# A graph kernel's gather on one core: VectorE's loop over six batches becomes a loop over two, and ScalarE copies finished tiles in a loop

## The reference

```python
# layer 1: gather rows of the features, weight, sum by destination
agg = segment_sum(layernorm(x)[src] * edge_weight[:, None], dst, 6250)
x = x + einsum('ni,oi->no', agg, W) + b
# layer 2: the half of the nodes with the largest router value go through gelu(sel @ w1 + b1) @ w2 + b2
x = x + ffn_of_chosen(layernorm(x))
# layer 3: 16 relations, each with its own 256x256 weight, a gate, then the same sum by destination
msg = einsum('nf,rfo->rno', h, weight)[rel_type, src] * norm * sigmoid(gate)
x = x + relu(segment_sum(msg, dst, 6250))
# layer 4: 8 experts of 256 -> 1024 -> 256, the top 2 of each node
x = x + experts(layernorm(x))
```

## Time and profile before

| | |
|---|---|
| device time, three runs | 4026.05, 4010.23, 4010.8 us; median 4010.8 us |
| profiled execution: span from first to last instruction | 3402.6 us (the page gives no other time of it) |
| between that span and the median of the runs | 608.2 us |
| instructions executed in the span | 59974 |
| PE, DVE, ACT, POOL busy | 2615.4, 1733.1, 723.6, 1869.7 us |
| granted TensorE clock, mean | 0.902 of full speed |
| the two gathers (POOL's first to last tile) | 78.7 to 1069.4 us, and to 2662.8 us for the second |

### The profile page before, as it was taken

The page is one execution under the profiler, slowest core; times in us unless marked ns, Lnnn a source line. Parts: engine busy times, 40 slices in busy tenths (PEclk is TensorE's granted clock), DMA queues, the critical chain, the costliest instruction groups (busy, mean ns, idle before and its releaser), DMA issues. The chain is left out here.

```text
span 3402.6 us, 59974 instructions
## 1 busy us (share of the span) xinstructions
PE 2615.4 (77%) x14271; PEld 1921.6 (56%) x14272; DVE 1733.1 (51%) x5663; ACT 723.6 (21%) x1907; POOL 1869.7 (55%) x1915
## 2 busy tenths in 40 slices
PE   7688888887777799999655555564555389999997
PEld 6577777776665344444344444443444267767774
DVE  6455545454554655555355454544544544545553
ACT  4121111111110233333211010000000233333332
POOL 1777777777774000000377777777777245555554
PEclk9899999998999899999888888777777689999998
DMA  7333333333332444444545454555544623222232
GB/s 224 110 113 113 113 111 111 113 113 113 110 113 67 173 197 192 188 191 194 194 141 155 151 154 142 152 154 151 146 146 146 241 59 48 45 45 48 45 48 33
DMA packets 175589, 434.08 MB, mean 128 GB/s; under 512 B 41712, under 2 KB 103792, under 8 KB 169232
## 3 DMA queue, kind: packets, MB, share of 16 engines
q0 software_dynamic: 97072, 236.21, 26.9%
q1 hardware_dynamic: 57424, 183.78, 14.1%
q10 hardware_dynamic: 21008, 13.24, 1.3%
HBM read 275.05 MB, written 158.04 MB: 127 GB/s over the span
## 5 line engine op out<-in xcount | busy, mean ns | idle before, releaser
L776 POOL DMA_INDIRECT g_msg<-table,idx x1564 | 1517.3, 970 | 518.8 <-issue 476.5
L848 PE MATMUL psum<-g_msg,g_hot 128*128 x3328 | 967.4, 456 | 593.0 <-SPq L719 358.1
L848 PEld LDWEIGHTS psum<-g_msg,g_hot 128*128 128x128 f32 x3328 | 756.5, 233 | 789.5 <-issue 654.5
L796 DVE TENSOR_SCALAR g_hot<-iota,g_cols 128x128 f32<-128x128 f32 x1664 | 450.1, 364 | 31.9 <-DVE g_cols L793 30.5
L1908 POOL DMA_INDIRECT out<-ex_y,ex_to x112 | 206.0, 1839 | 253.9 <-DMA out<-ex_y,ex_to 165.3
L768 POOL MEMSET g_origin<- 128x256 f32 x1 | 0.3, 313 | 590.8 <-POOLq L1359 590.8
L1594 PE MATMUL psum<-wrel_halves,t_xhi 128*128 128x512 f16 x784 | 298.2, 380 | 1.7 <-DVE t_row L1475 1.7
L1595 PE MATMUL psum<-wrel_halves,t_xhi 128*128 128x512 f16 x784 | 298.1, 380 | 0.0
L1596 PE MATMUL psum<-wrel_halves,t_xlo 128*128 128x512 f16 x784 | 298.1, 380 | 0.0
L1475 DVE TENSOR_SCALAR t_row<-psum,t_gate 128x256 f32<-128x256 f32 x392 | 171.2, 479 | 233.7 <-PE psum L1596 231.7
L2074 PE MATMUL psum<-w,ex_ghi 128*128 x784 | 260.6, 382 | 6.7 <-DVE ex_y L1983 6.4
(11 more groups left out here) (353 smaller groups left out, 3231.7 us busy)
## 6 DMA issues: line engine op xcount, KB each, us to landing
table<-t_row SPq DMA_DIRECT2D x48, 2048.0 KB, 6.3
g_msg<-table,idx POOLq DMA_INDIRECT x1564
piece_stage<-in_w SPq DMA_DIRECT2D x32, 512.0 KB, 5.7
w_halves<-piece_halves SPq DMA_DIRECT2D x32, 512.0 KB, 3.4
w<-w_halves SPq DMA_DIRECT2D x8, 2048.0 KB, 22.6
rows<-sc_row ACTq DMA_DIRECT2D x50, 128.0 KB, 2.2
out<-acc ACTq DMA_DIRECT2D x49, 128.0 KB
table<-t_row SPq DMA_DIRECT2D x24, 256.0 KB, 2.5
```

Source lines behind the costliest of these rows:

```text
L776: pool.indirect_dma_start(out=msg[:, at:at + D], out_offset=None, in_=table, in_offset=bass.IndirectOffsetOnAxis(ap=t[f"idx{g}"][:, n:n + ...
L796: last = nc.vector.tensor_scalar(hot[b][:, k * P:(k + 1) * P], t["iota32"][:, :], c3[:, k, where:where + 1], c3[:, k, weight:weight + 1], ...
L848: pe.matmul(ps, hot[b % PAIR][:, k * P:(k + 1) * P], msg[:, bass.ds(slot_at[k], D)], start=False, stop=False, skip_group_check=True).then_ ...
```

## The change

DVE's loop over the pieces becomes a loop of three turns within a loop: each inner turn makes two batches, runs one slot, and by two If tests halves the even piece in the first turn and the odd piece in the third. ACT's eight nested copies become one, under an If, and behind it a loop over the second to the eighth finished window, entered only where two or more windows have ended. Slot numbers are read with a load that tests its bounds on the chip. PE masks the two kinds of register value on which it waits with 1023.

```diff
     def slot_number(eng, m):
-        _, (n,) = nc.values_load_multi_w_load_instructions(slot_at(m, 0, 1), engines=[eng.engine], min_val=0, max_val=WINDOWS,
-                                                           skip_runtime_bounds_check_because=sure)
-        return n
+        return eng.value_load(slot_at(m, 0, 1), min_val=0, max_val=WINDOWS)
...
                 with dve.Fori(kind * turns, (kind + 1) * turns) as i:
-                    for k in range(2 * EACH):
-                        batch(2 * EACH * i + k, k % PAIR)
-                        if k % EACH == 1:
-                            pieces.halve(dve, kind, 2 * i + k // EACH, k // EACH)
-                        if k % 2:
-                            slots(dve, follow.vector, EACH * i + k // 2, tiles=True)
+                    with dve.Fori(0, EACH) as j:
+                        turn = EACH * i + j
+                        for b in range(PAIR):
+                            batch(PAIR * turn + b, b)
+                        with dve.If(j <= 0):
+                            pieces.halve(dve, kind, 2 * i, 0)
+                        with dve.If(j >= EACH - 1):
+                            pieces.halve(dve, kind, 2 * i + 1, 1)
+                        slots(dve, follow.vector, turn, tiles=True)
...
-                    pe.wait_ge(tiles_in, code[MSG_TILES])
+                    pe.wait_ge(tiles_in, code[MSG_TILES] & 1023)
                     for k in range(BATCH):
                         if k % BANKS == 0:
-                            pe.wait_ge(bank_free, code[BATCH + k // BANKS] + 1)
+                            pe.wait_ge(bank_free, (code[BATCH + k // BANKS] & 1023) + 1)
...
-            def close_from(k, m, start, end):
-                with act.If(end - start >= k + 1):
-                    _, (n,) = nc.values_load_multi_w_load_instructions(
-                        t["closed"][0:1, bass.ds(m, 1)], engines=[act.engine], min_val=0, max_val=WINDOWS - 1 - k,
-                        skip_runtime_bounds_check_because=sure)
-                    close(n + k)
-                    if k + 1 < BATCH:
-                        close_from(k + 1, m, start, end)
+            def close_all(m, start, end):
+                with act.If(end - start >= 1):
+                    n = act.value_load(t["closed"][0:1, bass.ds(m, 1)], min_val=0, max_val=WINDOWS - 1)
+                    close(n)
+                    with act.If(end - start >= 2):
+                        with act.Fori(1, BATCH) as k:
+                            with act.If(end - start - k >= 1):
+                                n = act.value_load(t["closed"][0:1, bass.ds(m, 1)], min_val=0, max_val=WINDOWS - 2)
+                                close(nc.s_assert_within(n + k, 0, WINDOWS - 1))
```

More of the change, by code:

```diff
@@ L895, in _ @@
                         t["closed"][0:1, bass.ds(m, 2)], engines=[act.engine], min_val=0, max_val=WINDOWS, skip_runtime_bounds_check_because=sure)
-                    close_from(0, m, start, end)
+                    close_all(m, start, end)
                 if follow:
```

## The result

| | before | changed |
|---|---|---|
| device time, median of four runs each on one chip | 4010.5 us (4004.6 to 4026.1) | 4074.3 us (4067.0 to 4082.7) |
| ratio, 95% interval | | 1.0162 (1.0135 to 1.0188) |
| profiled execution: device time, span | not given, 3402.6 us | 4082.7, 4080.8 us |
| granted clock, mean | 0.902 | 0.812 |
| instructions executed | 59974 | 61714 |

The change makes the kernel 64 us slower, 1.6%; I had forecast 4012.8. The profiled execution of the changed kernel is one of its timed runs, and its device time is its span and 1.9 us. So next to nothing lies around a span, and the trace of before that I read, at 3402.6 us, was not like the runs that I had set beside it.

A forecast was written before the change was run, and what follows sets the result against it. Prediction: POOL's issuing of indirect DMAs bounds both gathers; gather ends add +1.1 and +0.85, about +2 us, on the 3402.6 us span, giving 3404.6; with 608.2 carried over, 4012.8 us, range 4004 to 4022.

The forecast's parts named there:

- The sum's last step: Whole kernel: 608.2 us between profiled span and median run time, added unchanged to the forecast span of 3404.6 us.
- "to spare" figures: Gathers at POOL's pace: DVE has 6.3 us a turn, ACT waits 7.4 a copy, PE's release margin 3.6.
- the rival of 0.09: Around the span: the 608.2 us shrink with the program's 8.9% fewer instructions, -54 us, to 3957; chance 0.09.
- against 6.3 us to spare: 0: DVE's loop in the gathers: 0.8 us a turn added, hidden in 6.3 us of slack, cost 0.
- weighed the fetch: DVE's gather loop: old 236 instructions, now 98, not fetched again each turn, so a smaller loop gains 0.
- Net one ahead of the first matmul and one ahead of the fifth: PE's masks in each batch: register operations exposed 0.27 us a turn on 18.2, POOL stall taken as 0.
- forecast up to 30, under 6: Sign in the changed profile: SP's waits for PE before a release, up to 30 us in sum, each under 6.
- the slot number's check of 0.34: PE at gather 0's end: each of three loads that become checked costs 0.34 us with handovers.
- PE becomes the pace: Gather 0 turns: PE instead of POOL sets the pace, 20 us needing +1.8 us a turn, 4031; chance 0.05.
- +1.1 us at gather 0: End of gather 0: three checked loads, 1.0 us, plus 0.1 to 0.2 of masks delay PE's slot and first count.
- the 0.85 forecast: End of gather 1: three checked loads on ACT, 0.7 us, with PE's masks 0.85.
- ScalarE's loop: 0: ACT's copies: the new loop never runs; each close's checked load, some 0.24 us, hides in a 7.4 us wait.

The follow-up runs named there:

- unrolled_dve: Changed kernel with VectorE's loop over the pieces written out entirely, no loop: 3407.3 us, 1.0001 to the kernel before.
- old_both: Changed kernel with VectorE's old loop and ScalarE's old nested copies, keeping checked loads and PE's masks: 4093.6 us, 1.0102 to the kernel before.
- the four kernels on the chip with 3407: Changed kernel with additions on ACT or SP (three kernels) or VectorE's loop written out: 3430.3, 3428.2, 3429.6 and 3407.3 us.
- the three padded ones: Changed kernel plus semaphore increments on ACT in the gathers, increments on SP between them, or checked loads on ACT: 3430.3, 3428.2, 3429.6 us.
- changed_again: The changed kernel timed again without an edit: 4122.3 us, 1.0182 to the kernel before.
- old_dve_loop: Changed kernel with VectorE's old loop of six batches: 4090.0 us, 1.0090 to the kernel before.
- shift_14: Changed kernel with 14 never executed instructions in VectorE's program, so its later code stands 14 places on: 4058.6 us, 1.0135 to the kernel before.
- pad_act_third: Changed kernel with 24 spare semaphore increments at the end of each of ACT's 104 gather turns: 4221.4 us, 1.0412 to the kernel before.
- pad_pe_gather: Changed kernel with 24 spare semaphore increments in each of PE's 104 turns, ahead of the slot: 4471.5 us, 1.1044 to the kernel before.

## Why the prediction was wrong

**The sum's last step failed first.** "608.2 us lie between the span and the median of the runs, 4010.8, and I carry them over": they don't lie around a span. The changed kernel's span and its device time differ by 1.9 us, and so do those of every timed run of before whose span is listed. The trace was of an execution as on the chip with 3407 us; the timed runs were in the other regime. That before's own runs at 4005 to 4051 us have the 0.7 us steps, and that PE sets the pace in them, is concluded, not shown: every kernel profiled on those chips had them, and the steps of the changed kernel lie in code that the change doesn't touch. All "to spare" figures, and with them every cost put at 0, were of a regime that the forecast time doesn't belong to. For the same reason the rival of 0.09, a time around the span that shrinks with the program, had nothing to shrink.

**"against 6.3 us to spare: 0", the cost of VectorE's loop, failed.** Its running cost was hidden where POOL sets the pace (gather 0 takes 988.4 to 988.9 us with it, 989.6 without). In the slower regime the loop costs 29 to 37 us, of which the stage between the gathers has some 20 and "behind" 3.5; what is left isn't assigned. What wasn't in the sum is that 270 instructions fewer move all of VectorE's code behind it, and that a later loop of 397 then touches five fetched blocks and not four: 16 to 21 us between the gathers, shown in both directions. I had weighed the fetch only for the loop that the change makes smaller. The Trainium skill, page "Runtime: NRT & Kernel Launch", section "Instruction fetch mechanics", says that a taken jump to code outside the window waits for a fetch; the stalls once a turn behind the jump agree. The same section makes the window two blocks of 256, and here the places of the stops fit blocks of 128 alone: the measurement decides.

**PE's masks and the checked loads.** "Net one ahead of the first matmul and one ahead of the fifth", 0.27 us a turn, hidden: right where POOL sets the pace. PE's turn came to 18.5 (forecast 18.4 to 18.5), SP's waits for PE to 27.9 us, 18 times, at most 4.8 (forecast up to 30, under 6), and no row of POOL waits for SP. `unrolled_dve` there, with all checks and masks, is at 1.0001. Where the runs of the forecast lie, PE sets the pace, the cover is gone, and masks and checks cost 42 us in `old_both`. An estimate of their size from the traces: 104 turns at 0.3 us (the turn's growth on the chip with 3407 us) make 31, and 66 if the slot number's check of 0.34 is hidden there and exposed here; 42 lies between. How it divides over masks and checks, and over PE and the other engines, no run shows. So the rival "PE becomes the pace", at 0.05, named the mechanism; but by the conclusion above PE was it before the change too, and its turn had not to grow by 1.8 us.

**The ends of the gathers.** Of the +1.1 us at gather 0 some 0.4 are to be seen: from POOL's last tile to the first count 15.3 us before, 15.6 to 15.7 in the four kernels on the chip with 3407; from POOL's first tile it is 1006.0 before and 1004.1 to 1005.8 in them. "Behind" is 5 to 7 us longer in the three padded ones and 1.0 longer in `unrolled_dve`, so the checks' part is near the 0.85 forecast; the other 4 to 6 came with VectorE's loop and I haven't traced them.

**ScalarE's loop: 0.** Right, within the noise: 1.0180 against 1.0182.

The parts on the chip with 4051 us: checks and masks 42, VectorE's loop the other 29 (20 between the gathers and 3.5 behind them by the profiled executions), ScalarE's loop nothing to be told; together 71. On a chip with 3407 us the changed kernel itself never ran; its three padded forms put it at 3428 to 3430, 0.6 to 0.7% slower: the stop between the gathers, and the 4 to 6 us behind them that I haven't traced.

Open are four things: what differs between the chips or their state, and so what the 0.7 us steps are; why ACT's increments cost in gather 1 and not in gather 0; how the 42 us divide over masks and checked loads; and the 4 to 6 us behind the gathers. No version beat the kernel before.

## What to carry to other kernels

Before a trace is used for a forecast, its own time (span and what lies around it) has to be that of the timed runs; here a gap of 15% was another regime, in which another engine set the pace, and not a constant to add. A change that shortens an engine's program moves all code behind it: look for later loops of some hundred instructions on that engine, and whether they come to touch one block more; a few instructions in a branch that isn't taken move them back. An instruction that is hidden where POOL sets the pace has to be paid for on PE as soon as PE does (140 ns for each increment here).

## What was not expected of the hardware

The same program takes 3407 us on one chip and 4005 to 4051 on four others, with no row that names the reason. On those, in the gathers, sequencers show instructions that take 0.7 us or 1.4 us instead of tens of ns, and none in the stage between them. Dividing gather 0 by the instructions that the trace holds in it gives 80.9 ns (1473.7 us, 18213) in the changed kernel and 80.2 to 82.6 in `changed_again`, `old_dve_loop`, `old_both` and `shift_14`, and 82.3 to 85.3 in their gathers 1, where the mix of work is another; before's faster execution has 56.8 and 75.3. It is no fixed price of an instruction: in gather 0 `pad_act_third` has 76.5 and `pad_pe_gather` 85.9. The experts' stage executes some 26 instructions a us without a step, and gather 0 of the changed kernel 12, so it is not the rate of instructions alone. A stop of VectorE at the edge of a fetched block takes 5.0 to 5.7 us.
